# Attention and gated recurrence on one core: the softmax division moved from the token layout to the layout of the values product

## What is computed

```python
qkv = jnp.einsum('bse,fe->bsf', x, w_in)            # 16 heads of 16
p = jax.nn.softmax(scores, axis=-1)                 # own window and the one before
out = jnp.einsum('bhnqk,bhnkd->bhnqd', p, v2)
x = _layernorm(x + jnp.einsum('bse,fe->bsf', o, w_out))
ft = jax.nn.sigmoid(xt @ wf.T + c @ uf.T + bf)
it = jax.nn.sigmoid(xt @ wi.T + c @ ui.T + bi)
gt = jnp.tanh(xt @ wc.T + c @ uc.T + bc)
c = ft * c + it * gt
h = jnp.tanh(jnp.einsum('tbi,oi->tbo', x, wo) + c_final @ uo.T + bo)
x = _layernorm(x + h)
```

## Time and profile before

| what | value |
|---|---|
| median of 3 runs | 994.82 us (992.92 to 995.28) |
| the profiled execution, its own time | 994.83 us |
| span of that execution, first to last instruction | 992.7 us |
| mean granted clock of PE | 0.955 |
| busy: PE, DVE, ACT, POOL | 911.2, 714.1, 574.8, 409.0 us |
| DMA moved | 131.86 MB |

### The profile page before, as it was taken

How to read it: one execution, slowest core, us unless ns; L and a number is a source line. 1 busy time by engine, 2 the same in 40 slices (tenths; PEclk the granted TensorE clock), 3 DMA queues, 4 the chain that set the end, 5 groups by cost and what they waited for, 6 DMA issues and landing times. The chain is left out here.

```text
span 992.7 us, 25986 instructions
## 1 busy us (share of the span) xinstructions
PE 911.2 (92%) x9500; PEld 749.7 (76%) x9500; DVE 714.1 (72%) x2795; ACT 574.8 (58%) x1167; POOL 409.0 (41%) x687
## 2 busy tenths in 40 slices
PE   3587889999999999999999999999999999989994
PEld 2365668888888888888888888888787876668884
DVE  7666677878787868787878787878787754337875
ACT  6044556565656565656565656565656554335786
POOL 6143343444535353535353535354444443001443
PEclk8586989999999999999999999999999989899998
DMA  7644454535454545353645454645444400131764
GB/s 265 164 124 127 131 139 132 151 122 156 124 151 128 145 134 150 123 154 125 153 128 151 128 143 137 149 131 147 133 121 138 119 23 22 44 106 46 215 204 131
DMA packets 93534, 131.86 MB, mean 133 GB/s; under 512 B 12128, under 2 KB 47584, under 8 KB 93408
## 3 DMA queue, kind: packets, MB, share of 16 engines
q1 hardware_dynamic: 93136, 129.95, 45.3%
q10 hardware_dynamic: 272, 0.26, 0.1%
HBM read 79.31 MB, written 50.33 MB: 131 GB/s over the span
## 5 line engine op out<-in xcount | busy, mean ns | idle before, releaser
L689 DVE CUSTOM_DVE_ANT_0 bank<-bank,mask 128x256 f32<-128x256 f32 (+1 forms) x1024 | 369.4, 423 | 130.7 <-PE bank L951 128.7
L448 ACT ACTIVATE Pt<-bank 128x512 f32<-128x512 f32 (+1 forms) x512 | 248.2, 536 | 193.4 <-PE bank L972 193.3
L347 POOL TENSOR_SCALAR_AFFINE_SELECT Pt<-Pt 128x512 f32<-128x512 f32 x256 | 170.4, 666 | 403.9 <-ACT Pt L448 403.9
L951 PE MATMUL bank<-Ks,Qs 59*128 59x256 f32 (+1 forms) x1024 | 148.2, 319 | 44.9 <-DVE max_q L689 31.3
L951 PEld LDWEIGHTS bank<-Ks,Qs 59*128 59x128 f32 x1024 | 107.3, 191 | 86.6 <-DVE max_q L689 42.5
L689 DVE DVE_READ_ACCUMULATOR2_ANT max_q<- 128x1 f32 x1024 | 144.9, 142 | 0.0
L349 POOL TENSOR_SCALAR_AFFINE_SELECT Pt<-Pt 128x384 f32<-128x384 f32 x256 | 144.7, 565 | 0.0
L986 PE MATMUL bank<-Pt,Vp 128*32 128x256 f32 (+1 forms) x2048 | 130.9, 377 | 0.0
L932 PE MATMUL bank<-x1T,Wg 64*128 64x512 f32 x960 | 127.9, 398 | 1.0 <-DVE o_tok L703 1.0
L932 PE MATMUL bank<-cT,Ug 64*128 64x512 f32 x960 | 125.7, 393 | 0.0
L972 PE MATMUL bank<-Qs,Ks 60*128 60x256 f32 (+1 forms) x1024 | 111.8, 271 | 0.7 <-ACT Pt L448 0.3
(11 more groups left out here) (111 smaller groups left out, 1354.7 us busy)
## 6 DMA issues: line engine op xcount, KB each, us to landing
parts_dram<-qk_parts SPq DMA_DIRECT2D x128, 256.0 KB
Qs<-parts_dram SPq DMA_DIRECT2D x128, 128.0 KB, 2.7
Ks<-parts_dram SPq DMA_DIRECT2D x128, 128.0 KB, 2.8
xt_raw<-in_xt SPq DMA_DIRECT2D x16, 512.0 KB, 4.5
Qs<-parts_dram SPq DMA_DIRECT2D x128, 64.0 KB, 2.7
Ks<-parts_dram SPq DMA_DIRECT2D x128, 64.0 KB, 2.7
x_res<-in_x SPq DMA_DIRECT2D x16, 512.0 KB, 3.9
x_dram<-y SPq DMA_DIRECT2D x16, 512.0 KB, 4.4
```

Of the source, the lines that this page charges most:

```text
L347: gp.affine_select(out=p4[:, :, 0:128], in_=p4[:, :, 0:128], compare_op=ALU.is_ge, fill=0.0, base=0, pattern=[[0, 4], [1, 128]], channel_m ...
L448: sc.activation(probabilities(g, 2 * pair + odd)[:, S * a:S * a + n], SC[odd][:, 0:n], ACT.Exp).then_inc(exp_done, 1)
L689: ins = ve.tensor_tensor_reduce(out=raw, in0=raw, in1=mask[:, keys], scale=1.0, scalar=MASKED, op0=ALU.add, op1=ALU.max, accum_out=max_q[: ...
L951: ins = te.matmul(MX[odd][:, 256 * (n % 2):256 * (n % 2) + 256][:, keys], Qs[rows, 2 * g + pair, n * WIN:(n + 1) * WIN], Ks[rows, 2 * g + ...
```

## The change

For sequences 0 to 14 the division is done in the layout in which the values product leaves its result (features on partitions, tokens along the row). ACT copies the bank as before and issues a store of it to DRAM; SP loads the context rows of eight heads each into o_un and the denominators into den_q; DVE turns the denominators (transpose in blocks), inverts them and turns them back; SP stores the inverses and loads them spread over 16 rows a head into inv_den; POOL multiplies (scale_contexts). ot_hi and ot_lo now read o_un. The transposes of the context and of the output fall away. The last sequence keeps the old way (functions with last_ in the name).

With it: the second query/key pair is projected in slots 9 and 10 and the values in 11 and 12 (before: the other way round), with their pairs of banks; the x1 transposes stand ahead of the max transpose and the values in slot 13; x_hi is made at the end of the iteration before and x_lo is moved from DVE to POOL; x_res is loaded one iteration sooner, behind the max row of quad 0; the parts of chunk 1 are stored behind the rows of the next iteration; Wo and Uo are loaded and split in the last sequences, into space of Win. In the loop (shortened):

```diff
-        Uo = sb("Uo", [128, 2, KC, E], F32R)
 
...
+        den_q = sb("den_q", [128, 128])
+        den_t = sb("den_t", [128, 128])
+        last_o_tok = sb("last_o_tok", [128, NB, E])
         oT = sb("oT", [128, 2, KC, S], F32R)
 
...
         k_rows_raw = Pt[:, 5, 0:S]
 
...
+            def load_denominators(t):
+
+                sp.wait_ge(den_cleared, 1)
+                for g in range(QUADS):
+                    wait(sp, ctx_stored[g], 16, t, 16)
+                wait(sp, inv_stored, 16, t - 1, 16)
+                rows = ctx_dram[t % 2].rearrange("g (h r) (q i) -> q (g h) r i", r=2 * D, i=128)[:, :, D, :]
+                for q in range(4):
+                    sp.dma_start(den_q[32 * q:32 * q + H, :], rows[q]).then_inc(den_in, 16)
+
+            def load_contexts(t, c):
+                for g in (2 * c, 2 * c + 1):
+                    wait(sp, ctx_stored[g], 16, t, 16)
+                wait(sp, otlo_done, 2, t - 1, c + 1)
+                rows = ctx_dram[t % 2, 2 * c:2 * c + 2].rearrange("g (h r) s -> (g h) r s", r=2 * D)[:, 0:D, :]
+                sp.dma_start(o_un[:, c, :], rows).then_inc(o_un_in[c], 16)
+
+            def store_inverses(t):
+                wait(sp, inv_turned, 1, t, 1)
+                sp.dma_start(inv_dram[t % 2].rearrange("r (q i) -> q r i", i=128), den_q[:, :]).then_inc(inv_stored, 16)
+
+            def spread_inverses(t):
+
+                wait(sp, inv_stored, 16, t, 16)
+                for c in range(KC):
+                    wait(sp, scaled_done, 2, t - 1, c + 1)
+                    rows = inv_dram[t % 2, 8 * c:8 * c + 8]
+                    sp.dma_start(inv_den[:, c, :], rows.unsqueeze(1).to_broadcast([8, D, S])).then_inc(inv_in[c], 16)
+
...
+                by_rows = p1 and t - 1 < B - 1
                 if p1: max_to_stack(t - 1, 3)
-                if now: stack(t, 1)
-                if p2:
-                    wait(sp, y_done, 2, t - 3, 2)
-                    sp.dma_start(x_res[:, :, :], x[t - 2].rearrange(tok, p=128)).then_inc(xres_in, 16)
+                if now:
+                    stack(t, 1)
+                    if t: parts_to_dram(t, 1)
+                if by_rows: load_contexts(t - 1, 0)
                 if real(t + 2): load_xt(t + 2)
+                if now: max_to_stack(t, 0)
+                if p1:
+                    wait(sp, y_done, 2, t - 2, 2)
+                    sp.dma_start(x_res[:, :, :], x[t - 1].rearrange(tok, p=128)).then_inc(xres_in, 16)
                 if now:
                     stack(t, 2)
-                    max_to_stack(t, 0)
                     stack(t, 3)
                 if n1: parts_to_dram(t + 1, 0)
...
+                if by_rows: load_denominators(t - 1)
                 if n1: stack(t + 1, 0)
+                if by_rows: load_contexts(t - 1, 1)
                 if now: max_to_stack(t, 2)
-                if n1: parts_to_dram(t + 1, 1)
+                if by_rows:
+                    store_inverses(t - 1)
+                    spread_inverses(t - 1)
+                if t == B - 1: load_last_weights()
...
+            def scale_contexts(t, c):
+
+                wait(pool, o_un_in[c], 16, t, 16)
+                wait(pool, inv_in[c], 16, t, 16)
+                gp.tensor_tensor(o_un[:, c, :], o_un[:, c, :], inv_den[:, c, :], ALU.mult).then_inc(scaled_done, 1)
...
+                if p2 and t - 2 < B - 1:
+                    for c in range(KC):
+                        scale_contexts(t - 2, c)
...
+                    for hh in range(2):
+                        window(t, 1, hh)
+                    if real(t + 2):
+                        for c in range(KC):
+                            x_lo(t + 2, c)
+                    for hh in range(2, 4):
                         window(t, 1, hh)
...
             def ctx_out(t, g, bank):
                 wait(act, pv_ready, 4, t, g + 1)
-                wait(act, ct_ready, 4, t, g)
+                pt, pg = before(t, g)
+                if pt < B - 1:
+                    wait(act, ctx_stored[pg], 16, pt, 16)
+                else:
+                    act.wait_ge(ct_ready, g)
                 sc.activation(ctx_raw[:, :], bank[:, :], ACT.Copy).then_inc(ctx_done, 1)
-
-            def ot_hi(t, c, bank):
+                if t < B - 1:
+                    wait(act, ctx_done, 4, t, g + 1)
+                    sc.dma_start(ctx_dram[t % 2, g], ctx_raw[:, :]).then_inc(ctx_stored[g], 16)
+
+            def ot_hi(t, c):
                 if c == 0:
                     wait(act, op_ready, 2, t - 1, 2)
-                wait(act, ot_ready, 2, t, c + 1)
+                wait(act, scaled_done, 2, t, c + 1)
+                sc.activation(oT[:, 0, c, :], o_un[:, c, :], ACT.Copy).then_inc(othi_done, 1)
...
+                attend(1)
+                if t == 0: x_hi(1, 0)
                 if p2:
-                    ot_hi(t - 2, 0, B0)
-                    ot_hi(t - 2, 1, B1)
-                attend(1)
-                if n1: x_hi(t + 1, 0)
+                    ot_hi(t - 2, 0)
+                    ot_hi(t - 2, 1)
                 attend(2)
-                if n1: x_hi(t + 1, 1)
+                if t == 0: x_hi(1, 1)
...
+                if n1: qk_hi(t + 1, 2, A0)
                 attend(11)
-                v_out(t, 0, A0)
+                if n1: qk_hi(t + 1, 3, A1)
                 attend(12)
-                v_out(t, 1, A1)
-                if n1: qk_hi(t + 1, 2, B0)
-                max_row(t, 2, A0)
+                v_out(t, 0, B0)
+                v_out(t, 1, B1)
+                if p2: x1_hi(t - 2, 0, A0)
+                max_row(t, 2, B0)
                 attend(13)
-                if n1: qk_hi(t + 1, 3, B1)
-                ctx_out(t, 0, A1)
-                if p2:
-                    x1_hi(t - 2, 0, B0)
-                    x1_hi(t - 2, 1, B1)
+                if p2: x1_hi(t - 2, 1, A1)
+                ctx_out(t, 0, B1)
+                if real(t + 2): x_hi(t + 2, 0)
                 attend(14)
+                if real(t + 2): x_hi(t + 2, 1)
...
+            def turn_denominators(t):
+
+                wait(dve, den_in, 64, t, 64)
+                ve.transpose(den_t[:, :], den_q[:, :]).then_inc(den_turned, 1)
+
+            def invert_denominators(t):
+                wait(dve, den_turned, 1, t, 1)
+                own = den_t[:, :].rearrange("p (b r) -> p b r", r=32)[:, :, 0:H]
+                ve.reciprocal(own, own).then_inc(den_inverted, 1)
+
+            def turn_inverses(t):
+                wait(dve, den_inverted, 1, t, 1)
+                ve.transpose(den_q[:, :], den_t[:, :]).then_inc(inv_turned, 1)
+
+            def ot_lo(t, c):
+                wait(dve, othi_done, 2, t, c + 1)
+                minus_hi(oT[:, 1, c, :], o_un[:, c, :], oT[:, 0, c, :]).then_inc(otlo_done, 1)
...
-                if p1: normalise(t - 1, 0, A0)
+                if p3: forget(t - 3, 0)
+                attend(1)
...
                 if p2:
-                    ot_lo(t - 2, 0, B0)
-                    ot_lo(t - 2, 1, B1)
-                attend(1)
-                if n1: x_lo(t + 1, 0)
-                if p3: forget(t - 3, 0)
-                attend(2)
-                if n1: x_lo(t + 1, 1)
+                    ot_lo(t - 2, 0)
+                    ot_lo(t - 2, 1)
...
+                if n1: qk_lo(t + 1, 2, A0)
                 attend(11)
+                if n1: qk_lo(t + 1, 3, A1)
...
-                if n1: qk_lo(t + 1, 2, B0)
...
-                if n1: qk_lo(t + 1, 3, B1)
-                if p1: normalise(t - 1, 3, A0)
-                if p2:
-                    x1_lo(t - 2, 0, B0)
-                    x1_lo(t - 2, 1, B1)
+                if p1:
+                    turn_denominators(t - 1)
+                    invert_denominators(t - 1)
+                if p2: x1_lo(t - 2, 0, A0)
+                if p1: turn_inverses(t - 1)
+                if p2: x1_lo(t - 2, 1, A1)
...
+                if n1:
+                    q2, q3 = qk_halves(t + 1, 2, A0), qk_halves(t + 1, 3, A1)
+                    freed(pe, (gate_done, 6, t - 3, 5), (maxrow_done, 4, t, 1))
+                    freed(pe, (gate_done, 6, t - 3, 6), (ctx_done, 4, t - 1, 3), (qklo_done, 4, t, 2))
+                    abreast(q2, q3, 0, None)
+                attend(10)
+                if n1: abreast(q2, q3, 1, qk_ready)
+
+                attend(11)
+                v0, v1 = v_halves(t, 0, B0), v_halves(t, 1, B1)
+                wait(pe, maxrow_done, 4, t, 2)
+                freed(pe, (ctx_done, 4, t - 1, 4), (qklo_done, 4, t + 1, 2))
                 abreast(v0, v1, 0, None)
-                attend(10)
+                attend(12)
                 abreast(v0, v1, 1, v_ready)
...
                 attend(13)
+                if p2:
+                    freed(pe, (qklo_done, 4, t + 1, 3), (gate_done, 6, t - 3, 5))
+                    x1_transpose(t - 2, 0, A0)
+                    freed(pe, (qklo_done, 4, t + 1, 4), (gate_done, 6, t - 3, 6))
+                    x1_transpose(t - 2, 1, A1)
                 wait(pe, v_done, 2, t, 1)
```

(8 more changed lines are left out.)

225 lines of the change are left out of this document (114 added, 111 removed).

## The result

The changed kernel takes 1035.73 us (median of 4 runs, 1033.9 to 1039.98) beside 995.05 us for the kernel before in the same session: a ratio of 1.0418 (95% interval 1.0379 to 1.0457), slower. The forecast was 978 in a range of 955 to 1000.

A forecast was written before the change was run, and what follows sets the result against it. TensorE, busy 49.4 of 50 us, was taken as the bound. The terms -45.9 + 16.5 + 6.3 + 4.2 + 1.7 = -17.2 took 994.83 us to 977.6, stated as 978, range 955 to 1000.

The forecast's parts named there:

- Removed 45.9: TensorE, sequences 0 to 14: context and output transposes go, 3.06 us an iteration, 45.9 us in 15.
- second pair +16.5: Slots 9 to 12: second query/key pair's low parts delay maxima and raw scores, 1.1 us in 15 iterations, +16.5.
- gates of slot 14 +6.3: Slots 13 to 14: TensorE waits for ScalarE's context copy before slot 14's gates, 0.45 us in 14 iterations, +6.3.
- tail +1.7: End of kernel: three ScalarE weight copies of 0.60 stand ahead of sequence 14's copies and layer norm, +1.7 us.
- New transfers: ScalarE's and SyncE's queues: 1.9 and 4 us of issues, about 2.1 MB more an iteration; no term in the sum.
- Moved on SyncE: x_res and the max row ahead of stack(t, 2): SyncE's queue before slot 8: stack issued later, costing 0.3 us in 14 iterations with other shrunken slacks, +4.2.
- a landing takes 2.5 us in a quiet stretch and 5.5 behind a 512 KB load: Stack(t, 2) before slot 8: last issue at 487.5, so data there between 490 and 493.0; cost 0 to 0.4.
- From half busy to two thirds: DMA engines over an iteration: about 2.1 MB join 6.9 MB, raising how busy they are.
- The parts behind the rows cost nothing: SyncE's queue: moving chunk 1's parts costs 0, since only stack(t, 2) reads them.
- late transfers or masks: Rival: stack(t, 2) lands late or GpSimd's masks come late, 1 to 1.5 us an iteration, 992 to 999; chance 0.20.
- the raw scores of slot 8 released by a stack's transfer: Sign that the forecast is wrong: a stack's transfer releases the raw scores of slot 8 or 4.
- The clock falls: Rival: slot 12's pause drops TensorE's clock, slot 13 takes some 2.5 us more, 1013 us; chance 0.12.

The follow-up runs named there:

- e8: e6 without the division's transfers, so that the division works on ones; 975.23 us, ratio 0.98.
- e4: Changed kernel with none of the division's transfers made, its buffers holding ones, the order of the other loads kept; 1003.3 us, ratio 1.007.
- e6: Changed kernel with the second pair's parts back at the end of the iteration before and stack 2 right behind stack 1; 1057.32 us, ratio 1.0642.
- e7: Kernel before with only the second pair's parts issued an iteration later, behind the fourth maximum row and stack(t,1); 1033.28 us, ratio 1.0382.
- e5: Changed kernel with only the second pair's parts put back to the end of the iteration before, ahead of the inverses; 1099.03 us, ratio 1.1034.
- e10: Changed kernel with x_res loaded in the iteration that uses it, behind stack 1, as before the change; 1026.1 us, ratio 1.0316.
- e1: Changed kernel with the first o_un load, xt and x_res moved behind stack(t,2) in SP's queue; 1076.16 us, ratio 1.0793.
- e9: Changed kernel with the second pair's parts behind the spread of the inverses and stack 2 directly behind stack 1; 1034.53 us, ratio 1.0417.
- e17: e16 with row 1 ahead of the first pair's parts, o_un 0 ahead of that row, and x_res behind the spread; 1016.28 us, ratio 1.0202.
- e18: e17 with the denominators' four loads issued by ACT instead of SP; 1035.63 us, ratio 1.0411.
- e3: Changed kernel with the two o_un loads reading 128 whole consecutive rows (other values) instead of eight blocks of 16; 1023.28 us, ratio 1.0277.
- e13: e12 with the o_un loads from 128 whole consecutive rows of other values; 994.16 us, ratio 0.9988.
- e12: Changed kernel with xt, o_un 0 and x_res behind x_dram, and stack 2 directly behind the parts; 1028.34 us, ratio 1.0364.
- e16: e12 with o_un's load and the spread as 16 blocks of eight rows, and the inverses' store in four pieces; 1006.55 us, ratio 1.0105.

## Why the prediction was wrong

- *The engines' terms were right in sum.* Removed 45.9, second pair +16.5, gates of slot 14 +6.3, tail +1.7 make 973.4 without the transfers' 4.2; e8, which has all of that work on the engines and no stack late after the start, took 975.23. One by one: from slot 10 to slot 13 it is 477.11 - 469.43 = 7.68 us, where the earlier trace rows give 506.20 - 499.58 = 6.62, so 1.06 against 1.1 (499.58 is slot 10's start in the trace of before); the waits stand where foretold, on max_q. Slot 14's gates wait 0.26 against 0.45, and the tail's layer norm 5.6 where 3.99 and +1.7 were put. Part of the agreement is luck: e8 reaches its first x1 transposes 4.5 us later than the kernel before (164.13 against 159.58 us), for which the sum has nothing, and the last of its iterations is 4.8 us shorter (45.87 against 50.66), more than the sum gives it.
- *The step that failed* stands in two passages. "New transfers" gave the division's transfers no term, and "Moved on SyncE: x_res and the max row ahead of stack(t, 2)" gave all lateness "0.3 in 14 iterations: +4.2". Against these 4.2 the runs show 1035.7 - 975.2 = 60.5 us. By e4 and e8 it parts into 32.4 for the division's transfers in this order (1035.7 - 1003.3) and 28.1 for the order with those transfers away (1003.3 - 975.2); the two are no separate prices, since in the order of e6 the same transfers cost 82 (1057.3 - 975.2). About a third of the 60.5 is not waiting: for the same 9140 instructions TensorE is busy 891.8 us in the changed kernel, at a mean clock of 0.935, and 872.3 in e8, at 0.948.
- *What was wrong in that step is the landing.* The issues are where it put them: in the iteration shown the stack goes out 8.7 to 4.0 us before slot 8 was due (463.40 - 4.54 = 458.86), the forecast was 8.3 to 4.6. But "a landing takes 2.5 us in a quiet stretch and 5.5 behind a 512 KB load", and the last of the stack's eight transfers took 8.9 from the start of its issue, behind o_un, xt, the parts and x_res (the other seven 4.8 to 6.1). "From half busy to two thirds" was right as a mean (0.63) and no help: from 449 to 463 us the engines are at 0.95 to 1.12, and at 473 to 475 at 0.05.
- *Two sentences beside it.* "The parts behind the rows cost nothing" asked only who reads them, not what is queued behind: e7 prices it at 38 us in the kernel before. In the changed kernel the old place is worse still, by 63 us (e5, 1099.0 - 1035.7), since there the inverses stand behind the parts. And x_res sooner costs 10 us at its new place (e10).
- *Rival "late transfers or masks"* named the mechanism, stack(t, 2) behind x_res, at 1 to 1.5 us an iteration; it was 4.2 (577.28 us from the x1 transposes at 216.59 to those at 793.87, 11 iterations of 52.5, against 48.2 in e8). Of the signs of being wrong, the raw scores of slot 8 released by a stack's transfer is the one that came. PE waited 2.6 us in all for masks. *"The clock falls"* came true as a consequence only: not behind slot 12's pause of 0.42 us, but behind slot 8's of 4.5.
- *Still open:* whether an order exists in which all deadlines hold. Thirteen further kernels that divide in full were tried; where a late transfer was mended (e1, e6, e9, e17), another came late. Without the division's transfers such an order exists (e8).

The Trainium skill's sentence that transfers of all queues share 16 engines (Trainium Kernel Development and Optimization, Key Constraints) fits e18, where the second queue brought the denominators no sooner.

## What to carry to other kernels

Price a transfer by the DMA share of the stretch between its issue and its reader, not by the mean (and not by it alone: in e6 a store was held in a half-busy stretch), and write down for every transfer in a queue who reads it and when, before one is moved: behind a moved transfer stands all the rest. When a change takes work from the bound engine and adds a round trip through DRAM, a run without the transfers tells how much is there to be won and how much they may cost; here it took the old order as well (e8), since without the transfers alone (e4) a part of the loss stayed. A wait of some us on TensorE cost more than its length, since the work behind it ran at half clock: 2.98 us for 29 matmuls that took 1.68 elsewhere.

## What had not been expected of the hardware

- The DMA share does not tell the rate: in the changed kernel 0.99 was 323 GB/s at 451 us, with xt and x_res under way, and 1.12 was 148 GB/s at 455 us, with the stacks.
- The shape of a 256 KB load, with the same bytes, moved the time by 12 us in one order (e3) and by 34 in another (e13 beside e12).
- The length of an issue is not fixed: two rows of maxima took 1.37 us of SP's queue at 447.88 in the changed kernel and 3.67 at 505.34 in e16; one issue on ACT took 0.32 to 2.17 us (e18). How busy the engines were does not tell which: the share was 0.67 over the 1.37 us and 0.66 over the 3.67. The long one stands right behind the parts' issues; the reason stays open.
